# Rank-decayed sum of a graph kernel: weights kept in PSUM and halved at each edge, in place of counting the edges behind each

## The reference

```python
support = input @ weight
mask = (adj != 0).astype(support.dtype)
rank = jnp.cumsum(mask, axis=1)
deg = rank[:, -1:]
k = jnp.minimum(deg, float(MAX_NEIGH))          # MAX_NEIGH = 100
pos = rank - (deg - k)
w = mask * jnp.where(pos > 0, DECAY ** (k - pos), 0.0)   # DECAY = 0.5
out = w @ support + bias
```

## Time and profile before

| what | value |
|---|---|
| median of three runs | 2627.26 us |
| the profiled execution | 2625.25 us |
| its span in the profile | 2623.5 us |
| TensorE (PE), VectorE (DVE), ScalarE (ACT) busy | 2146, 1647, 769 us |
| read from memory, written | 698.7 MB, 135.3 MB |
| mean granted TensorE clock | 0.917 of full |
| last layer, from its first operation to the end | 2338 to 2623.5 us |

### The profile page before, as it was taken

One profiled execution on the slowest core, in us unless ns is written; L12 is line 12 of the kernel. 1 busy time (PEld: TensorE's weight loads), 2 busy tenths in 40 slices (PEclk: granted clock), 3 DMA queues, 4 the chain that ended last, 5 costly groups with the idle time before them and its releaser, 6 DMA issues. The chain is left out here.

```text
span 2623.5 us, 36440 instructions
## 1 busy us (share of the span) xinstructions
PE 2146.1 (82%) x15204; PEld 748.1 (29%) x15224; DVE 1647.2 (63%) x1785; ACT 768.6 (29%) x856; POOL 4.1 (0%) x16
## 2 busy tenths in 40 slices
PE   6769879799776566799999799776666799969998
PEld 2224243232221111244453233221111244432222
DVE  7870043288698888755523288698888755555553
ACT  0010010166443333111110166443333111125554
POOL 0000000000000000000000000000000000000000
PEclk9999989999887887899999999887887899979999
DMA  9958989799389898977779799389898977747770
GB/s 387 424 251 360 408 345 424 321 378 373 145 352 375 357 363 354 375 258 258 274 312 427 323 380 378 152 358 378 356 362 353 369 258 258 285 197 257 262 272 28
DMA packets 119369, 836.03 MB, mean 319 GB/s; under 512 B 8512, under 2 KB 10560, under 8 KB 76608
## 3 DMA queue, kind: packets, MB, share of 16 engines
q1 hardware_dynamic: 117184, 832.63, 80.4%
q10 hardware_dynamic: 2048, 1.35, 0.2%
HBM read 698.68 MB, written 135.27 MB: 318 GB/s over the span
## 5 line engine op out<-in xcount | busy, mean ns | idle before, releaser
L786 DVE CUSTOM_DVE_ANT_0 stream<-ps,stream 128x1024 f32<-128x1024 f32 x504 | 594.3, 1221 | 134.8 <-DMA stream<-in_adj 92.6
L797 ACT ACTIVATE stream<-stream,negmax 128x4096 f32<-128x4096 f32 x128 | 474.9, 3710 | 594.9 <-DVE negmax L791 594.9
L753 PE MATMUL ps<-edgeT,node_twice 64*128 64x512 f32 x1024 | 294.4, 699 | 253.1 <-DVE mx L786 253.1
L401 PE MATMUL ps<-stream,stage 128*64 128x512 f32 x1792 | 401.8, 599 | 62.1 <-DMA stream<-in_adjT 36.5
L1118 DVE SCALAR_TENSOR_TENSOR stream<-stream,cut 128x4096 f32<-128x4096 f32 x62 | 278.0, 4484 | 6.3
L753 PE MATMUL ps<-edgeT,query_twice 64*128 64x512 f32 x1024 | 245.4, 612 | 6.4 <-DVE edgeT L817 3.9
L1078 PE MATMUL ps<-stream,xw 32*64 32x512 f32 x4096 | 229.5, 589 | 0.6 <-ACT xw L1161 0.6
L753 PEld LDWEIGHTS ps<-edgeT,node_twice 64*128 64x128 f32 x1024 | 98.7, 210 | 440.6 <-DVE mx L786 330.4
L401 PEld LDWEIGHTS ps<-stream,stage 128*64 128x64 f32 x1792 | 127.0, 138 | 330.2 <-issue 285.1
L768 PE MATMUL ps<-stream,ones 128*1 128x512 f32 x1024 | 181.0, 844 | 8.2 <-DVE stream L1118 8.2
L1343 ACT ACTIVATE stream<-ps,bits_bias 128x1024 int32<-128x1024 f32 x128 | 142.4, 1114 | 108.1 <-PE ps L1308 107.2
(11 more groups left out here) (180 smaller groups left out, 1461.7 us busy)
## 6 DMA issues: line engine op xcount, KB each, us to landing
stream<-in_adj SPq DMA_DIRECT2D x178, 2048.0 KB, 11.8
stream<-in_adjT SPq DMA_DIRECT2D x74, 2048.0 KB, 12.2
pruned<-stream SPq DMA_DIRECT2D x64, 2048.0 KB, 7.7
spare<-pruned SPq DMA_DIRECT2D x22, 2048.0 KB, 11.2
query_twice<-pruned SPq DMA_DIRECT2D x22, 2048.0 KB, 11.4
node_twice<-pruned SPq DMA_DIRECT2D x20, 2048.0 KB, 11.5
query_twice<-in_adjT SPq DMA_DIRECT2D x7, 2048.0 KB, 35.3
node_twice<-in_adjT SPq DMA_DIRECT2D x7, 2048.0 KB, 35.2
```

The source lines that it names most:

```text
L401: last = nc.tensor.matmul(ps[F * h:F * h + F, bank + b, :], stage[:, t.k % SL, :], half_bank(src, b, h), start=False, stop=False, skip_gro ...
L753: last = nc.tensor.matmul(ps[:, 2 * slot + h, :], stationary[F * h:F * h + F, rows_n], bank_of(edgeT[F * h:F * h + F, :], c), start=True, ...
L786: nc.vector.tensor_tensor_reduce(out=prod[s][:, cols], in0=ps[:, 2 * slot:2 * slot + 2, :].rearrange("p a b -> p (a b)"), in1=block_in[:, ...
L797: nc.scalar.activation(prod[s], prod[s], ACT.Exp, bias=negmax[:, s:s + 1], accum_out=zsum[:, s:s + 1]).then_inc(exp_done, 1)
```

## The change

The last layer no longer counts. Four PSUM banks hold, for half of the columns (2048) and each of the 128 partitions, twice the weight of the next edge. A unit is one half of one row block; there are 64, the first half of the columns through all blocks, then the second. For each of its four chunks of 512 columns ScalarE reads the bank, takes one from the exponent by integer arithmetic (with 0 as its floor) and writes it to SBUF; VectorE multiplies that by "is an edge" and gives bf16 weights; TensorE subtracts these weights from the bank with a negated identity, so an edge halves its entry, and then adds weights times features. The features are split by VectorE into three bf16 parts whose sum they are, so a chunk takes three products for each half of the partitions in place of one f32 product. A load now brings two half blocks, with 8 KB in a piece.

For one partition to see only its own edges, nodes are laid out anew: partition p holds nodes 32p to 32p+31, one in each block. What an entry starts from is the number of edges in later partitions. It comes from a bf16 tally of 4096 columns per partition: VectorE counts blocks 24 to 31 in `l0`, where its column sum now ends with block 24 and TensorE makes the column sums of the last 8 blocks itself, and blocks 0 to 23 in `l1`. In `i0_edge` TensorE turns the tally into counts, ScalarE into the bits of a power of two in bf16, and its queue stores them (1 MB); GpSimd waits for the store. The end of the last `prune` reads them back, ahead of the first four loads of `l3`. The loops of `l0` and `l1` are written out in place of a repeated body.

The diff, cut to its core (of the last layer only what is new; its loops before are in the section above, and go):

```diff
+        tally = edgeT[:, :].bitcast(BF16)
...
+        starts_kept = nc.dram_tensor("row_starts", (P, N), BF16, kind="Internal").ap()
...
+        def count_edges(v, src, first):
+            if first:
+                return v.tensor_scalar(tally, src, 0.0, None, ALU.not_equal)
+            return v.scalar_tensor_tensor(out=tally, in0=src, scalar=0.0, in1=tally, op0=ALU.not_equal, op1=ALU.add)
...
+            on_vector = [*range(summed), *counted]
+            first_on_vector = on_vector[0] if on_vector else 0
+            assert on_vector in ([], [*range(first_on_vector, NB)])
+            def every_block(e, body):
+                if on_vector:
+                    for n in range(NB):
+                        body(last_step(n, seq))
+                else:
+                    row_blocks(e, SL, lead, body, seq)
...
-                    if column_sums:
-                        wait(sp, added, t.n - (SL - 1))
+                    if on_vector:
+                        wait(sp, added, t.n - (SL - 1) - first_on_vector)
...
+                    if column_sums and t.k >= summed:
+                        for c in range(8):
+                            g, j = c % 4, c // 4
+                            last = nc.tensor.matmul(ps[32 * g:32 * g + 1, 4 + j, :], ones[:, :], column_sums(src, c),
+                                                    start=t.k == summed, stop=False, skip_group_check=True)
...
-                    pe.wait_ge(added, NB)
+                    pe.wait_ge(added, summed)
                     for c in range(8):
                         g, j = c % 4, c // 4
                         nc.tensor.matmul(ps[32 * g:32 * g + 1, 4 + j, :], ones[:, :],
-                                         column_sums(spare_block, c), start=True, stop=True)
-            if not column_sums:
+                                         column_sums(spare_block, c), start=False, stop=True, skip_group_check=True)
...
+                for n in on_vector:
+                    t = last_step(n, seq)
+                    src = slot[slots[n % SL]]
+                    if n >= resident:
+                        dve.wait_ge(loaded[n % SL], 16 * (t.turn(SL, resident) + 1))
+                    wait(dve, added, n - first_on_vector)
+                    if n in counted:
+                        count_edges(v, src, column_sums and n == counted[0]).then_inc(added, 1)
...
+            def count_after(half):
+                def count(pe):
+                    if half == 0:
+                        pe.wait_ge(q_taken, 2)
+                    else:
+                        pe.wait_ge(starts_made, 4)
+                    for c in range(4):
+                        for h in range(2):
+                            last = nc.tensor.matmul(ps[F * h:F * h + F, c, :], after_b[:, F * h:F * h + F],
+                                                    bank_of(tally, 4 * half + c), start=True, stop=True)
+                    last.then_inc(starts_counted, 1)
+                return count
+            def make_starts(half):
+                def make(act):
+                    act.wait_ge(starts_counted, half + 1)
+                    for c in range(4):
+                        nc.scalar.activation(bank_of(tally, 4 * half + c).bitcast(I16), ps[:, c, :], ACT.Relu,
+                                             bias=start_bias[:, :], scale=-float(ONE_EXPONENT_B))\
+                            .then_inc(starts_made, 1)
+                    if half == 1:
+                        act.wait_ge(starts_made, 8)
+                        act.dma_start(starts_kept, tally).then_inc(starts_stored, 16)
+                return make
+            if with_starts:
+                @block.gpsimd
+                def _(pool):
+                    pool.wait_ge(starts_stored, 16)
...
+            starts_side = {7: count_after(0), 9: count_after(1)} if with_starts else {}
+            starts_scalar = {8: make_starts(0), 10: make_starts(1)} if with_starts else {}
...
-                do(v.scalar_tensor_tensor(out=after_b[:, :], in0=ident[:, :], scalar=-float(NOT_EDGE),
-                                          in1=after[:, :], op0=ALU.mult, op1=ALU.add))
-                do(v.tensor_scalar(carry_b[:, :], after_b[:, :], -1.0, 1.0, ALU.mult, ALU.add))
+                do(v.tensor_copy(after_b[:, :], after[:, :]))
+                do(v.tensor_scalar(neg_ident_b[:, :], ident[:, :], -1.0, None, ALU.mult))
...
+                       summed=24, counted=range(24, NB))
...
+                       seq=[*range(24, NB), *range(24)], slots=range(8), resident=8, counted=range(8, NB))
...
+            edge_pass(block, sem, res, [(x_ready, k + 1) for k in range(4)], with_starts=True)
...
+        def half_blocks(m):
+            half, k = divmod(m, HB)
+            pair = adjT_b[NB - 2 - 2 * k:NB - 2 * k]
+            return pair.rearrange("n p c -> p n c")[:, :, HALF * half:HALF * half + HALF]
+        def two_half_blocks(s):
+            return stream[:, s, :].rearrange("p (n c) -> p n c", n=2)
...
+                    if last_it:
+                        sp.wait_ge(gathered, groups * CH)
+                        sp.dma_start(starts, starts_kept).then_inc(next_ahead[4], 16)
                     for done, slots_free in ((groups - 1, (2, 3)), (groups, (0, 1))):
                         sp.wait_ge(scattered, done)
                         for s in slots_free:
-                            sp.dma_start(stream[:, s, :], adjT_b[NB - 1 - s] if last_it else adj_b[s]).then_inc(next_ahead[s], 16)
+                            if last_it:
+                                sp.dma_start(two_half_blocks(s), half_blocks(s)).then_inc(next_ahead[s], 16)
+                            else:
+                                sp.dma_start(stream[:, s, :], adj_b[s]).then_inc(next_ahead[s], 16)
...
+            SL, QC = 4, 4
+            units = 2 * NB
+            loaded, starts_loaded = next_ahead[0:SL], next_ahead[SL]
+            clean = q2[:, 0:HALF]
+            weight = [q2[:, HALF:N].bitcast(BF16)[:, HALF * i:HALF * i + HALF] for i in range(2)]
+            support = [stream[:, 5, :].bitcast(BF16)[:, HALF * i:HALF * i + HALF].rearrange("p (n f) -> p n f", f=F)
+                       for i in range(3)]
             @block.sync
             def _(sp):
...
+                for m in range(SL, NB):
+                    sp.wait_ge(weighed, 2 * QC * (m - SL + 1))
+                    sp.dma_start(two_half_blocks(m % SL), half_blocks(m)).then_inc(loaded[m % SL], 16)
                 for k in range(4):
                     sp.wait_ge(out_made, k + 1)
                     sp.dma_start(part(d["out"], k), part(cur, k)).then_inc(out_stored, 16)
                 sp.wait_ge(out_stored, 64)
+            @block.scalar
+            def _(act):
+                norm.root(act)
+                for u in range(units):
+                    for c in range(QC):
+                        act.wait_ge(decay_ready, QC * u + c + 1)
+                        nc.scalar.activation(bank_of(clean, c).bitcast(I32), ps[:, c, :].bitcast(I32), ACT.Relu,
+                                             bias=less_one_exponent[:, :], scale=1.0).then_inc(cleaned, 1)
+                    if u == 0:
+                        act.wait_ge(fold_ready, 1)
+                        nc.scalar.copy(curT[:, :], fold4b).then_inc(fold_taken, 1)
+                        act.wait_ge(sup_ready, 1)
+                        nc.scalar.copy(support[0], nat4b).then_inc(sup_taken, 1)
+                out_norm.scalar(act, nat4)
             @block.vector
             def _(dve):
                 v = nc.vector
                 do = Chain(dve, chain)
                 norm.scale(dve, do, res, res, x_ready)
...
+                for u in range(units):
+                    m = u // 2
+                    if u % 2 == 0:
+                        dve.wait_ge(loaded[m % SL], 16 * (m // SL + 1))
+                    wait(dve, summed, u - 1)
+                    edges = two_half_blocks(m % SL)[:, 1 - u % 2, :]
+                    for c in range(QC):
+                        dve.wait_ge(cleaned, QC * u + c + 1)
+                        v.scalar_tensor_tensor(out=bank_of(weight[u % 2], c), in0=bank_of(edges, c), scalar=0.0,
+                                               in1=bank_of(clean, c), op0=ALU.not_equal, op1=ALU.mult)\
+                            .then_inc(weighed, 1)
+                    if u == 0:
+                        dve.wait_ge(sup_taken, 1)
+                        do(v.tensor_tensor(cur[:, :, :], nat4b, support[0], ALU.subtract))
+                        do(v.tensor_copy(support[1], cur[:, :, :]))
+                        v.tensor_tensor(support[2], cur[:, :, :], support[1], ALU.subtract).then_inc(sup_split, 1)
+                dve.wait_ge(summed, units)
                 for b in range(4):
                     c = slice(BANK * b, BANK * b + BANK)
                     v.scalar_tensor_tensor(out=accT[:, c], in0=fold4b[:, c], scalar=b3[:, :], in1=curT[:, c],
...
             @block.tensor
```

(45 more changed lines are left out.)

128 lines of the change are left out of this document (34 added, 94 removed).

## The result

| what | before | after |
|---|---|---|
| median | 2627.56 us (4 runs, 2624.27 to 2629.78) | 2544.59 us (4 runs, 2542.96 to 2547.16) |
| ratio | | 0.9686, 95% interval 0.9669 to 0.9703 |
| the profiled execution, its span | 2625.25, 2623.5 us | 2542.96, 2541.2 us |
| VectorE, TensorE, ScalarE busy | 1647, 2146, 769 us | 1773, 2064, 785 us |

A forecast was written before the change was run, and what follows sets the result against it. TensorE was taken to bound the last stage's loop. Terms -88.4 (last layer), +4.8, +1.5 and +2.5 sum to -79.6: 2625.25 becomes 2545.7 profiled, 2547 forecast for the median, range 2528 to 2582.

The forecast's parts named there:

- rival A: Last layer's loop: VectorE's product pitch of 0.603 sets the pace, 2.45 us a unit taken; run at 2547, chance 0.60.
- B: Last layer's loop: the ScalarE, VectorE, TensorE ring or its handovers decide, 2.92 us a unit, +30, 2577; chance 0.22.
- TensorE, 10 pairs of 0.215: New loop: 20 64-wide bf16 products a unit run side by side in 10 pairs, 2.15 us.
- ScalarE, 2.1 to 2.36: New loop: ScalarE's four 512-column operations from PSUM take 2.1 to 2.36 us a unit.
- DMA at 424 GB/s from half rows: Last layer's loads: 8 KB half rows come as fast as whole rows, 4.95 us for two units.
- C: Last layer's loop: loads decide, at 385 GB/s; +6, run at 2553; chance 0.10.
- The start: Last layer before its steady loop: unit 1 starts at 2360.4 after the split, its third chunk waits +0.5.
- First layer: TensorE's column sums for the last 8 blocks make each block 5.45 us; +4.8, without switching +2.6.
- Second layer: VectorE counts 24 blocks at a pitch of 4.53 and ends last, at 332.5; +1.5, bounds +0.8 and +2.5.
- First edge pass: The 1 MB store adds +2.5 because the DMA engines are full; the added matmuls and ScalarE operations are absorbed.
- The moved loads "cost nothing": Loads ahead of the last layer, moved behind the last gather, are consumed after 2341 and so cost nothing.
- Rival D: New loop: TensorE's clock drops while waiting for products and TensorE becomes the bound; +115, 2662, slower than before; chance 0.06.

The follow-up runs named there:

- run 3: Changed kernel with ScalarE making the halving's input for only 256 of each chunk's 512 columns in the last layer; 2546.32 us.
- run 4: Changed kernel with VectorE forming weights for only 256 of each chunk's 512 columns in the last layer; 2542.35 us.
- run 8: Changed kernel with the features split into two bf16 parts instead of three, four products per sum instead of six; 2539.46 us.
- run 5: Changed kernel with ScalarE and VectorE both working on only 256 of each chunk's 512 columns; 2534.39 us.
- run 6: Changed kernel with a sum's six products ordered three for one half of the partitions, then three for the other; 2542.94 us.
- run 7: Changed kernel with all six products of a sum written to partitions 0 to 63; 2617.78 us.
- run 9: Changed kernel without TensorE's first-layer column sums of blocks 25 to 31; 2539.10 us.
- Run 1: Changed kernel with the first two loads ahead back behind sum 7, the starts read behind the last sum; 2542.60 us.

## Why the prediction came true, point by point

The mechanism held: the new loop's pace is VectorE's, and the loop is where the time was won. That the sum came within 2.7 us of span is in part luck, since a term that was put at nothing cost 2.8 and several others were too high by as much as 2.5.

**VectorE's pitch (rival A, a chance of 0.60): right.** 0.603 from the earlier trace rows is 0.602 in the loop, without the 0.01 for handovers that the 2.45 a unit contained: 63 x 0.04 = 2.5 us less. Runs 3, 4 and 8 show that the engine and not the ring decides, and in the loop the price of B is not paid even in part.

**TensorE, 10 pairs of 0.215: right in size, wrong in its reason.** 2.16 a unit in run 5. The prediction had read "side by side" off a row of eight in 1.05 us and took them for neighbouring pairs. Runs 6 and 7 show two streams, one for each half, that fill up wherever the products stand.

**ScalarE, 2.1 to 2.36: right**, 2.32 in run 4. **DMA at 424 GB/s from half rows: right**; 4.97 a pair in runs 4 and 5, 417 to 421 GB/s where it decides, against the 4.95 that were taken. C, at 385, falls. It is close behind, though: run 4's loop, 4% faster, met it.

**The start: two errors that cancel.** The projection came out 1.8 us shorter than its row, by luck: its granted clock was 1.00 in this execution and 0.66 in that row, and it took 5.28 or more in eight of the ten executions of this order. The wait after unit 0 was 1.53 + 0.93 = 2.46, not 0.5: the step assumed that only a third chunk waits behind one sum, but unit 0's sums run at the low clock after 7.32 us of idle, 1.49 for six instead of 0.81, and each of unit 1's halving products stands behind one of them. The unit's pitch above and these two are the terms of the last layer that were mis-sized by more than 1 us. Refill 2.06 against 1.9 and the end 1.02 against 1.0 were right. Together -1.8 + 2.0 - 2.5 + 0.2 = -2.1, which is the difference between -88.4 and -90.5.

**First layer: right in mechanism, 0.5 high.** A block takes 142.76 - 137.35 = 5.41 against 5.45 taken and 5.17 without a cost for switching, so if that estimate is right, some 0.24 a block is left for switching between the 64-wide and the one-wide products (the two costs that the prediction read off rows, 0.2 and 0.15, would make it 5.52 and not 5.45), and run 9 gives the whole 4.3 back when the sums go. **Second layer:** VectorE ends last, at 331.72 + 4.42 = 336.14, as forecast, 0.8 and not 1.5 later; its pitch of 4.53 was right, but it was free for the counts 0.8 sooner after the first layer's end than before (43.9 us and 44.7). **First edge pass:** the store was to cost 2.5. The stretch grew by 1.1, while the projection at its start ran 1.2 shorter than before (5.46 and 6.68 us for the same 32 products), so 2.3 is the store's. The trace bears the split out: from the phase's start to its first block's products it is 32.75 us before and 31.54 now, and from there to the last block's 136.05 and 138.31. No run left the store out.

**The moved loads "cost nothing": wrong, +2.8.** The step looked at who needs the data and how late it may come, and at SP's queue, and found cover for both. It did not ask what runs beside the transfers. Before, the loads lay beside the gather and behind the scatter; moved, they lie on top of the scatter, whose issue stops for 1.8 us, most likely for a fetch of instructions behind the loads, and whose rest is somewhat slower (197 products in 11.38, where 200 took 10.93 in the scatter ahead of it). Run 1 takes exactly that back.

**Rival D: false here.** The clock is 1.00 from 2371 to 2524; the first two units alone ran at 0.51, which is in the start's terms. The Trainium skill's rule (TensorE: Matmul & The Clock Gate, "A second HAM failure mode: psum-queue depth-cycling") would have had the clock swing in a loop of 512-column bf16 products that cycles through banks with small idle pieces; this loop is of that kind, and the trace does not agree with it. Even run 5, where TensorE waits for VectorE at every pair of loads, stays at 1.00 from 2371 to 2516.

## What to carry to other kernels

When one engine's work is spread over three, take each engine's pitch from a queued row of the same shape, price each resource as if it stood alone, and let the largest decide; the handovers of four chunks in flight cost nothing here at 97% use. After such a change the next bounds lie close together (VectorE 2.41, ScalarE 2.32, DMA 2.48 less what is read ahead, TensorE 2.16 a unit), so making the bound faster alone wins next to nothing. And when a transfer is moved, ask what it lands on top of, an engine's instructions and perhaps the program's own fetches, and not only when its data is needed.

## What the hardware showed that was not expected

- 64-wide products into different halves of the partitions overlap across TensorE's list, whatever their order and whatever lines they are from. The cost is 0.216 us times the larger of the two halves' counts: 16 steps, 3.45 us a unit, when the lower half has 16 of 20 products, 10 steps when they are even. A product for one half may start ahead of earlier ones for the other, and the semaphore mark still came when both were done. The Trainium skill (TensorE: Matmul & The Clock Gate, "The mechanism") states that matmuls start and end in strict program order; the starts in run 7 and the pace in run 6 don't agree, the marks do.
- TensorE's scatter stops issuing for 0.7 to 1.8 us when 2 MB loads start ahead of it, in ten executions of ten, and in none of the four without these loads. The length of the stop follows the landing of one 16 KB fetch of instructions, which comes 1.9 to 3.1 us behind the scatter's first product with the loads and 0.4 to 0.9 ahead of it without. That the fetch is the cause is likely and not shown.
- The same 32 products of the projection took 3.84, 5.28, 5.5 or 6.66 us in different executions, with the same instructions ahead of them. The granted clock over them was 1.00, 0.71, 0.68 to 0.69 and 0.55.
